# Causal attention heads on two 64-row halves of the array, with the products of the halves in turn to different PSUM banks

## The reference

```python
def _L1_attn_ref(x, w_qkv, w_out):              # 16 heads of 16 dimensions, x is [8, 256, 256]
    qkv = (x @ w_qkv).reshape(batch, seq_len, 3, NUM_HEADS, HEAD_DIM)
    ...
    q = q * cos + _rotate_half(q) * sin
    k = k * cos + _rotate_half(k) * sin
    scores = jnp.einsum('bhqd,bhkd->bhqk', q, k) * HEAD_DIM ** (-0.5)
    scores = jnp.where(causal, -jnp.inf, scores)
    probs = jax.nn.softmax(scores, axis=-1)
    out = jnp.einsum('bhqk,bhkd->bhqd', probs, v)
    ...
    return out @ w_out
t = _to_tokens(x)
t = t + _L1_attn_ref(_ln_t(t), L1_attn_w_qkv, L1_attn_w_out)
t = t + _L1_ffn_ref(_ln_t(t), L1_ffn_gate_w, L1_ffn_expert_w)
```

## Time and profile before

| | us |
|---|---|
| median of three runs | 736.01 |
| the profiled execution, its own time | 737.27 |
| its span, first to last instruction | 735.5 |
| mean granted TensorE clock in it, share of full speed | 0.93 |

### The profile page before, as it was taken

The page is one execution under the profiler, slowest core; times in us unless marked ns, Lnnn a source line. Parts: engine busy times, 40 slices in busy tenths (PEclk is TensorE's granted clock), DMA queues, the critical chain, the costliest instruction groups (busy, mean ns, idle before and its releaser), DMA issues.

```text
span 735.5 us, 20279 instructions
## 1 busy us (share of the span) xinstructions
PE 622.5 (85%) x8800; PEld 530.3 (72%) x8800; DVE 468.2 (64%) x1032; ACT 345.9 (47%) x549; POOL 247.5 (34%) x258
## 2 busy tenths in 40 slices
PE   6748899999989899564897788898989898988867
PEld 5636878888878788353785656687878787877755
DVE  2577769686777787213664525586868686867445
ACT  5454546363637463127875225444454535361610
POOL 1010111213030303004985417373645454543430
PEclk9869999999999999686998868799999999999997
DMA  7203001011010000002213031121304040300000
GB/s 280 80 3 128 16 3 55 4 54 41 16 69 3 2 3 3 1 0 57 64 32 66 29 43 44 31 60 29 70 20 73 16 74 16 74 16 1 16 15 16
DMA packets 16889, 29.78 MB, mean 40 GB/s; under 512 B 1952, under 2 KB 10400, under 8 KB 15904
## 3 DMA queue, kind: packets, MB, share of 16 engines
q1 hardware_dynamic: 16800, 28.49, 15.3%
HBM read 22.19 MB, written 6.29 MB: 39 GB/s over the span
## 4 chain that ended last, share of the span: by engine, by line
PE 36%; DVE 9%; ACT 5%; POOL 3%; issue 2%; DVEq 0%; POOLq 0%; ACTq 0%
PE ps L203 20%; DVE mx L1419 3%; PE ps L1150 3%; PE ps L1102 3%; PE ps L1128 2%; PE ps L1131 2%; PE ps L1013 2%; PE ps L1134 1%; PE ps L1105 1%; POOL hl L1328 1%; DVE acc L1509 1%; DVE st L1358 1%; ACT prob L1267 1%; ACT wide L1238 1%; DVE t L1464 1%
## 5 line engine op out<-in xcount | busy, mean ns | idle before, releaser
L1342 POOL TENSOR_TENSOR e2l<-prob,e2h 128x1536 f16<-128x1536 f32 x32 | 98.7, 3103 | 20.2 <-ACT e2h L1273 20.2
L203 PE MATMUL ps<-secondh,ch_moe 128*128 128x256 f16 (+1 forms) x320 | 82.5, 265 | 3.4 <-DVE cl_moe L1369 3.1
L203 PE MATMUL ps<-secondl,ch_moe 128*128 128x256 f16 (+1 forms) x320 | 82.8, 265 | 0.0
L203 PE MATMUL ps<-secondh,cl_moe 128*128 128x256 f16 (+1 forms) x320 | 82.7, 265 | 0.0
L1419 DVE TENSOR_REDUCE mx<-ps 128x2 f32<-128x512 f32 (+1 forms) x96 | 65.5, 682 | 26.1 <-PE ps L1105 26.0
L520 PE MATMUL ps<-yh,wconvh 128*128 128x240 f16 (+2 forms) x288 | 78.3, 272 | 4.0 <-POOL yl L676 4.0
L676 POOL TENSOR_TENSOR yl<-y,yh 128x128 f16<-128x128 f32 x32 | 12.6, 427 | 198.6 <-ACT yh L626 198.6
L520 PE MATMUL ps<-yh,wconvl 128*128 128x240 f16 (+2 forms) x288 | 78.2, 271 | 0.0
L520 PE MATMUL ps<-yl,wconvh 128*128 128x240 f16 (+2 forms) x288 | 78.1, 271 | 0.0
L1267 ACT ACTIVATE prob<-ps 128x1536 f32<-128x1536 f32 x32 | 46.5, 1452 | 47.9 <-PE ps L1134 47.9
L1509 DVE SCALAR_TENSOR_TENSOR acc<-ps,gate,acc 128x256 f32<-128x256 f32 x112 | 49.0, 479 | 27.3 <-PE ps L203 27.3
(11 more groups left out here) (220 smaller groups left out, 2082.8 us busy)
## 6 DMA issues: line engine op xcount, KB each, us to landing
weights_stage<-in_second SPq DMA_DIRECT2D x6, 684.0 KB, 4.1
qs<-rope_scratch SPq DMA_DIRECT2D x24, 128.0 KB, 3.7
ks<-rope_scratch SPq DMA_DIRECT2D x24, 128.0 KB, 5.5
weights_stage<-in_wconv SPq DMA_DIRECT2D x6, 384.0 KB, 4.4
xw<-in_xw SPq DMA_DIRECT2D x8, 256.0 KB, 2.7
xc<-in_xc SPq DMA_DIRECT2D x8, 256.0 KB, 2.7
rope_scratch<-rh SPq DMA_DIRECT2D x8, 256.0 KB, 2.3
rope_scratch<-rl SPq DMA_DIRECT2D x8, 256.0 KB, 2.3
```

Of the source, the lines that this page charges most:

```text
L203: last = nc.tensor.matmul(out_ap, lhs[x], rhs[w], start=done == 0, stop=done == n - 1)
L1342: nc.gpsimd.tensor_tensor(el[n % 2][:], prob[n % 2][:], eh[n % 2][:], ALU.subtract).then_inc(e2_lo, 1)
```

## The change

Queries and keys of heads 0 to 7 (in a new order of the heads, `ROW_HEADS`) now lie on partitions 0 to 47 and those of heads 8 to 15 on partitions 64 to 111, eight heads side by side; 16 zero rows fill each half to 64. Products of scores therefore run over 64 rows, in the lower or the upper half of the array. `maxima` takes its four heads from one half. `attend` takes two heads of each half: its sixteen products of scores and shifts stand in a fixed order in which the halves write to different banks at any time; before the third bank passes from one half to the other, PE waits for its own sixth product (`upper_rows`). The three products with the mask follow at the end, over 128 rows. The shifts of a half lie in the 16 rows of that half, so `headb`, `mxs` and `shift` change their layout, PE transposes the maxima into 128 rows instead of 32, and `mxs` is zeroed once instead of `shift`. SP copies each part of queries and keys in two halves.

The order of the steps is now spelled out for each engine in tables of letters (`WINDOW_ORDER`, `IMAGE_ORDER`) in place of the slots; the letters give each engine the steps that it had, in the order that it had. A few waits are named apart: `second_split` for the second weights, and waits in front of statistics, `weigh` and the first expert.

The diff, cut to what touches the causal attention:

```diff
+ROWS = P // 2
+L1HALF = L1H // 2
+ROW_HEADS = [4 * (h % L1HALF // 2) + 2 * (h // L1HALF) + h % 2 for h in range(L1H)]
...
+IMAGE_ORDER = {
...
+    "pe": (
+        "ttmtmwtmwntmwntmqwnrtmwrntmwvnmqwanaarawranaaaavaanasqeaeaaraereaiaiaaavaiaaiosqeuaeaaracelrxeaixaxi"
...
-        qs, ks = pair("qs", [KROWS, L1H, TOK], f16), pair("ks", [KROWS, L1H, TOK], f16)
+        qs, ks = pair("qs", [P, L1HALF, TOK], f16), pair("ks", [P, L1HALF, TOK], f16)
...
-        mxs = one("mx2s", [P, TILES, 2, L1H])
+        by_half = lambda t: t[:].rearrange("p t (g h) -> p t g h", g=2)
+        mxs = one("mx2s", [P, TILES, P])
+        mxs_parts = mxs[:].rearrange("p t (g r) -> p t g r", g=2)
...
-                        sp.dma_start(t[KSTACK:KROWS], a["zeros"].rearrange("p (h t) -> p h t", h=L1H))\
-                            .then_inc(rows_zeroed, 16)
+                        for half_rows in R2:
+                            r0 = half_rows * ROWS
+                            sp.dma_start(t[r0 + KSTACK:r0 + ROWS], a["zeros"].rearrange("p (h t) -> p h t", h=L1HALF))\
+                                .then_inc(rows_zeroed, 16)
...
-                        src = scratch[p, part, qk * 2:qk * 2 + 2].rearrange("j (d h) t -> (j d) (h t)", h=L1H)
-                        sp.dma_start(dst[p][n * L1D:(n + 1) * L1D].rearrange("r h t -> r (h t)"), src)\
-                            .then_inc(stacked[p], 16)
+                        src = scratch[p, part, qk * 2:qk * 2 + 2].rearrange("j (d h) t -> (j d) h t", h=L1H)
+                        for half_rows in R2:
+                            r0 = half_rows * ROWS + n * L1D
+                            sp.dma_start(dst[p][r0:r0 + L1D], src[:, half_rows * L1HALF:(half_rows + 1) * L1HALF])\
...
+            def row_half(h):
+
+                g = h // L1HALF
+                return slice(g * ROWS, (g + 1) * ROWS), h % L1HALF
...
-                    nc.tensor.matmul(to[:, m * keys:(m + 1) * keys], qs[p][:, gr * GH + h, q0:q0 + P],
-                                     ks[p][:, gr * GH + h, 0:keys], start=m == 0, stop=False)
+                    rows, at = row_half(gr * GH + h)
+                    nc.tensor.matmul(to[:, m * keys:(m + 1) * keys], qs[p][rows, at, q0:q0 + P],
+                                     ks[p][rows, at, 0:keys], start=m == 0, stop=False)
...
-                    last = nc.tensor.transpose(bank(1, 1)[0:2 * L1H, t * P:(t + 1) * P],
-                                               mxs[:, t].rearrange("p s h -> p (s h)"), ident)
+                    last = nc.tensor.transpose(bank(1, 1)[:, t * P:(t + 1) * P], mxs[:, t, :], ident)
...
-                for b, (heads, k0, q0) in enumerate(WEIGHT_BANKS):
-                    to, width = bank(0, b), TOK - q0
-                    for n, h in enumerate(heads):
-                        nc.tensor.matmul(to[:, n * width:(n + 1) * width], ks[p][:, gr * GH + h, k0:k0 + P],
-                                         qs[p][:, gr * GH + h, q0:TOK], start=n == 0, stop=False)
-                    for n, h in enumerate(heads):
-                        nc.tensor.matmul(to[:, n * width:(n + 1) * width], headb[:, gr * GH + h, :],
-                                         shift[p][:, q0:TOK], start=False, stop=False)
-                    diagonal = to.rearrange("p (h m) -> p h m", m=width)[:, :, 0:P]
+
+                def part(b, n):
+                    heads, k0, q0 = WEIGHT_BANKS[b]
+                    width = TOK - q0
+                    rows, at = row_half(heads[n] // 2 * L1HALF + gr * 2 + heads[n] % 2)
+                    return bank(0, b)[:, n * width:(n + 1) * width], rows, at, k0, q0
+
+                def scores(b, n, first=False):
+                    to, rows, at, k0, q0 = part(b, n)
+                    nc.tensor.matmul(to, ks[p][rows, at, k0:k0 + P], qs[p][rows, at, q0:TOK], start=first, stop=False)
+
+                def less_maxima(b, n):
+                    to, rows, at, k0, q0 = part(b, n)
+                    return nc.tensor.matmul(to, headb[rows, rows.start // ROWS * L1HALF + at, :], shift[p][rows, q0:TOK],
+                                            start=False, stop=False)
+
+                scores(2, 0, first=True)
+                scores(1, 0, first=True)
+                scores(2, 1)
+                less_maxima(2, 0)
+                scores(1, 1)
+                less_maxima(2, 1).then_inc(upper_rows, 1)
+                scores(0, 0, first=True)
+                less_maxima(1, 0)
+                scores(0, 1)
+                less_maxima(1, 1)
+                pe.wait_ge(upper_rows, c * GROUPS + gr + 1)
+                less_maxima(0, 0)
+                scores(2, 2)
+                scores(2, 3)
+                less_maxima(0, 1)
+                less_maxima(2, 2)
+                less_maxima(2, 3)
+                for b, (heads, _, q0) in enumerate(WEIGHT_BANKS):
+                    diagonal = bank(0, b).rearrange("p (h m) -> p h m", m=TOK - q0)[:, :, 0:P]
                     last = nc.tensor.matmul(diagonal, identb[:], laterb[:].unsqueeze(1).to_broadcast([P, len(heads), P]),
                                             start=False, stop=True)
                 last.then_inc(weights2, 1)
...
+                if gr == 0:
+                    pe.wait_ge(v2_lo, c + 1)
...
-                if e == 1:
+                if e == 0:
+                    pe.wait_ge(n3_lo, c + 1)
+                elif e == 1:
...
-                    for p in R2:
-                        nc.gpsimd.memset(shift[p][:], 0.0).then_inc(shift_set, 1)
+                    nc.gpsimd.memset(mxs[:], 0.0).then_inc(shift_set, 1)
...
+                    freed(dve, ln["mv"][m], c)
...
-                nc.vector.tensor_tensor(mxs[:, :, 1, :], mx[c % 2][:], mxh[:], ALU.subtract).then_inc(mx_step, 1)
+                nc.vector.tensor_tensor(mxs_parts[:, :, :, L1HALF:L1H], by_half(mx[c % 2]), by_half(mxh), ALU.subtract).then_inc(mx_step, 1)
                 dve.wait_ge(mx_step, c * 3 + 2)
-                nc.vector.tensor_tensor(mxs[:, :, 0, :], mx[c % 2][:], mxs[:, :, 1, :], ALU.subtract)\
+                nc.vector.tensor_tensor(mxs_parts[:, :, :, 0:L1HALF], by_half(mx[c % 2]),
+                                        mxs_parts[:, :, :, L1HALF:L1H], ALU.subtract)\
                     .then_inc(mx_step, 1)
...
-                nc.vector.tensor_copy(shift[c % 2][0:2 * L1H, :], bank(1, 1)[0:2 * L1H, 0:TOK])\
+                nc.vector.tensor_copy(shift[c % 2][:], bank(1, 1)[:, 0:TOK])\
...
-    put("head", np.where((row % L1H == head) & (row < 2 * L1H), -1.0, 0.0))
+    in_half = row - ROWS * (head // L1HALF)
+    put("head", np.where((in_half % L1HALF == head % L1HALF) & (in_half >= 0) & (in_half < L1H), -1.0, 0.0))
...
-    order = lambda m: m.reshape(C, L1H, 2, 8).transpose(0, 2, 3, 1).reshape(C, C)
+    order = lambda m: m.reshape(C, L1H, 2, 8)[:, ROW_HEADS].transpose(0, 2, 3, 1).reshape(C, C)
```

More of the change, by code:

```diff
@@ L158, with turns, in_order @@
+def turns(step, parts):
+    for c in range(B):
+        for part in parts or ((),):
+            yield step, c, part
+def in_order(order, steps):
+    left = {letter: turns(step, parts) for letter, (step, *parts) in steps.items()}
+    for letter in order:
+        step, c, part = next(left[letter])
+        step(c, *part)
 MLP, QKV, MOE = range(3)
 IN_MLP = 4
-MLP_SLOT = [
-    ("load", 0), ("widen", 4), ("mlp_normalise", 2), ("mlp_base", 2), ("mlp_low", 3), ("narrow", 5),
-    ("statistics", 5), ("tokens", 1), ("mlp_channels", 2)]
@@ L306, in step_of, with run @@
             return c % 2, c // 2
-        def run(steps):
-            for name, c, *which in window_order():
-                if name in steps:
-                    steps[name](c, *which)
+        def run(engine, steps):
+            in_order(WINDOW_ORDER[engine], steps)
         def behind(eng, semaphores, c, n):
@@ L953, in images, with run @@
              "expert_done", "acc_done", "half_set2", "ones_set2"))
-        head_set, shift_set = sem("head_set"), sem("shift_set")
-        order = image_order()
-        def run(steps):
-            for name, c, *which in order:
-                if name in steps:
-                    steps[name](c, *which)
+        head_set, shift_set, upper_rows = sem("head_set"), sem("shift_set"), sem("upper_rows")
+        def run(engine, steps):
+            in_order(IMAGE_ORDER[engine], steps)
         flat = lambda t: t[:].rearrange("p h t -> p (h t)")
@@ L1001, in store @@
                 sp.dma_start(out[c * P:(c + 1) * P], acc[c % 2][:]).then_inc(stored[c % 2], 16)
-            run({"load": load, "stack": stack, "store": store})
+            run("sp", {
+                "l": (load,), "s": (stack,), "t": (store,)})
             for p in R2:
@@ L1347, in _ @@
             pool.wait_ge(half_set, 3)
-            run({"tokens": deviation(MLP), "mlp_base": mlp_base, "widen": widen, "statistics": deviation(QKV),
-                 "moe_statistics": deviation(MOE), "stack": stack, "rotated_low": rotated_low, "split": split})
+            run("pool", {
```

(5 more changed lines are left out.)

167 lines of the change are left out of this document (83 added, 84 removed).

## The result

The changed kernel takes 743.25 us (median of four runs, 742.61 to 743.51), the kernel before 735.89 in the same comparison: a ratio of 1.0106, with a 95% interval of 1.0062 to 1.015. A second comparison gave 742.92 and 1.0122 (1.0086 to 1.0159). It is about 1% slower.

A forecast was written before the change was run, and what follows sets the result against it. PE was taken to bound the kernel (busy 85% of the span). Attend -10.7, maxima +11.9 and +0.3 off the chain gave +1.5 us on the median of 736.01: 737.5 us predicted, range 724 to 752.

The forecast's parts named there:

- the likeliest case: Whole kernel: time within 1% of the kernel before, own range 731 to 743 us, chance 0.55.
- Attend: Score and shift products on two halves side by side: 0.44 us saved each at full clock, 10.7 us on the chain.
- Maxima: Steps with all heads in one half: two switches, 0.20 us lost in a stream, 0.10 behind a wait, 11.9 us total.
- The copies and the other waits: 12 copies of 64 KB instead of 6 of 128 KB, and new waits on past events: nothing, copies 0.9 us at most.
- An image without a fall: One image of the attention's middle stage (481 to 641 us): about 36.2 us, up from about 35.5.
- What is saved there becomes idle time: The 11 attends off the chain end in a wait for DVE, so their saving counts nothing.
- the sum: Whole kernel: 10.7 us saved in attend, 11.9 lost in maxima, 0.3 for maxima off the chain: +1.5 us.
- The first rival: Switches between whole and half array cost only 0.03 us: 10 us faster, 726 us; chance 0.18.
- the third: Products of unequal width in the two halves do not overlap in attend: 753 us; chance 0.05.
- The second: Weights of a product in the same half don't load behind the one before: 0.02 to 0.09 us each, 743 to 761; chance 0.22.

The follow-up runs named there:

- the split attend with useless work: Changed kernel with maxima back on all rows and group 1's three mask products in attend issued twice: 725.58 us (0.9881), again 724.86 us (0.9869).
- attend's halves in turn: Changed kernel with attend's sixteen products reordered so that one half of the array follows the other: 747.6 us, 1.0136 of the kernel before.

## Why the prediction was right or wrong

The time lies in the range, and 6 us above the predicted one; the likeliest case, within 1%, was narrowly missed: the ratio is 1.0106, and 743.25 lies at the upper end of that case's own range, 731 to 743.

- Attend. Forecast 0.44 us saved at full clock; measured 1.76 - 1.33 = 0.43, and 0.06 less where the output projection follows and waits for DVE, a wait that the prediction did not have. Alone, the split attend gained 8.8 and 6.4 us in two comparisons, falls behind the wait included, for a term of 10.7; since the clock of 390 to 481 us was higher in its profiles too, this nearness is in part luck. The pairs, the two switches and the wait on upper_rows came as laid out (the wait costs 0.01: starts at 612.73 and 612.85 are 0.12 apart, where 256 columns take 0.11).
- Maxima. Right: 0.2 a step, and 11.5 us in the kernel with this part alone, for a term of 11.9.
- The copies and the other waits. Nothing, as taken; no transfer is waited for.
- An image without a fall. Forecast 36.2 us, measured 36.43.
- The step that failed is "What is saved there becomes idle time", read as costing nothing, and with it the clock, which was allowed for in 390 to 481 us alone. The attends off the chain were saved for nothing, as it said; but the idle time that they left brought the clock of the middle stage, which had not once fallen, to 0.97. Three falls of about 1.3 us are some 4 us. The prediction named a clock under 1.00 there among the things that would make it wrong, and gave it no price.
- With that idle time filled, the change is worth 1.003 of before, 1.6 us: the sum had +1.5. The interval (0.9998 to 1.0062) spans nearly 5 us and the useless products take time of their own, so the near equality is in part luck.
- The first rival (cheap switches) falls by the 0.20 at 632.07, and the third by the pairs. The second (weights of the same half not hidden) falls by the 0.06 a product of four products of one half in a row, from 537.79 to 538.03, each with a weight load of 0.09. The rule of the Trainium skill (TensorE: Matmul & The Clock Gate, part 3) that weight loads overlap only in another row group would have made them longer; the trace disagrees with it here too.

The accounts close as follows, by PE's timeline of the changed kernel (first) and of the one before. From the first maxima step (399.00) to an attend at 478.36 the changed kernel takes 79.4 us, the kernel before 82.6:

```profile
399.00 0.28 PE L1114 MATMUL ps<-ks,qs 64*128 64x128 f16 x2
...
478.36 0.28 PE L1145 MATMUL ps<-qs,ks 64*128 64x128 f16 x3
```

```profile
399.42 0.31 PE L1102 MATMUL ps<-ks,qs 80*128 80x128 f16 x1
...
481.98 0.38 PE L1128 MATMUL ps<-qs,ks 80*128 80x256 f16 x2
...
645.01 0.27 PE L1128 MATMUL ps<-qs,ks 80*128 80x256 f16 x1
```

In the second profiles it is 79.8 and 82.5. Two attends that ran at half clock before are among these 3 us, and the clock of the stage is higher; that they belong to the kernels is not shown by two profiles of each, since those of the split attend with useless work, one kernel, differ by 5 us in the same stretch (73.8 and 78.8). From there to the attend at 649.73 (before: 645.01) it is 171.4 against 163.0 us: 8.3 us lost, where the forecast of 0.7 an image makes 3.3. The three falls are some 4 of them, the changed products, at 0.9 an image, the rest. Behind it another 1.4 us is lost: in the last image the clock falls from 657.5 to 665 us in both profiles of the changed kernel, in the kernel before not until 684.

Open stays why an image falls and the next one, with the same wait, doesn't. Idle time is part of it: adding it slows the kernel before and lets the clock of its last image fall, filling it speeds up the changed one. It is not all: 0.68 us with attend over all rows left the clock alone, and 0.45 us with attend's halves in turn came with two falls, where 0.44 with the maxima on all rows came with none. Whether attend's narrower use of the array, the place of the waits within the image or the moment at which they come makes the difference, no run here tells apart.

## What to carry to other kernels

Work that leaves an engine just ahead of one of its waits is not simply free: look at what the granted clock does behind that wait, and price a fall from a stretch at either level. Packing two halves of the array pays where independent products of both halves stand close to each other; steps with all their products in one half only pay the two switches, 0.2 us here, so give them an operand that is zero in the other half and leave them on all rows. Count the switches per step before the columns saved.

## What the runs showed of the hardware

- PE runs products of the other half ahead of its queue: the two scores of bank 1 began before the two shifts of bank 0 that stand ahead of them, and the four products of each bank ran beside the other's (538.03 to 538.48).
- A fall of the clock lasts some 3.5 to 4 us in the middle stage and up to 14 us elsewhere (454 to 468 us in the kernel before), and a useless 0.43 us of products ahead of a wait can cost less than the falls that it prevents (737.97 against 743 us).
- The switch between all rows and half of them costs some 0.10 us into the half and 0.10 back, at full clock, in the maxima step as in the window stage (632.07 to 632.59, 292.15 to 292.35).
- With PE idle for 0.80 us instead of 0.37 ahead of two more waits of 0.8, the clock behind them fell in both profiles (0.77 and 0.89 from 645 to 660 us); in both of the kernel before it stayed at 1.00.
